# Splitting the product with C of a state-space scan between VectorE and GpSimd, and moving the gathers on GpSimd

## The reference, cut to what matters

```python
dA = jnp.exp(dt_t[..., None] * A)
h = dA * h + (dt_t * u_t)[..., None] * B_t[:, None, :]
y_t = jnp.einsum('bdn,bn->bd', h, C_t)
```

## Time and profile before

| what | value |
|---|---|
| median of three runs | 618.16 us (617.43 to 618.87) |
| the profiled execution | 619.79 us, its span 618.2 us |
| TensorE busy, its weight loads | 414.6 us, 206.4 us |
| VectorE busy | 477.4 us (77%) |
| ScalarE busy | 204.3 us (33%) |
| GpSimd busy | 351.2 us (57%) |
| from 125 to 345 us (most of the scan): VectorE busy | 209.6 of 220 us |

### The profile page before, as it was taken

One profiled execution on the slowest core, in us unless ns is written; L12 is line 12 of the kernel. 1 busy time (PEld: TensorE's weight loads), 2 busy tenths in 40 slices (PEclk: granted clock), 3 DMA queues, 4 the chain that ended last, 5 costly groups with the idle time before them and its releaser, 6 DMA issues.

```text
span 618.2 us, 8775 instructions
## 1 busy us (share of the span) xinstructions
PE 414.6 (67%) x3283; PEld 206.4 (33%) x3283; DVE 477.4 (77%) x625; ACT 204.3 (33%) x229; POOL 351.2 (57%) x307
## 2 busy tenths in 40 slices
PE   6786855757676677767767889687163996545751
PEld 2462323222232222222222345475132434522220
DVE  1999998799999999999998328999406469994242
ACT  2565992222323323333331355321011126112110
POOL 6667004569999999998998232889980000330000
PEclk7978976679999999999999999855556997567567
DMA  8540033925545475456440000000010000000000
GB/s 283 176 138 9 2 91 74 227 71 150 160 143 155 142 173 137 136 159 177 141 136 1 2 12 1 2 2 2 1 22 1 1 0 1 2 2 8 4 5 34
DMA packets 29523, 46.11 MB, mean 75 GB/s; under 512 B 18146, under 2 KB 19588, under 8 KB 28452
## 3 DMA queue, kind: packets, MB, share of 16 engines
q1 hardware_dynamic: 27044, 45.12, 26.7%
q0 software_dynamic: 2368, 0.37, 0.5%
q10 hardware_dynamic: 64, 0.00, 0.0%
HBM read 43.57 MB, written 1.11 MB: 72 GB/s over the span
## 4 chain that ended last, share of the span: by engine, by line
DVE 31%; POOL 31%; PE 20%; issue 12%; ACT 3%; DMA 2%; DVEq 1%; ACTq 0%; POOLq 0%; SPq 0%
POOL dBu L888 14%; POOL hit L872 7%; PE ps L2015 4%; POOL work L965 3%; POOL work L967 3%; DVE hC L1552 2%; PE ps L2338 2%; POOL work L954 2%; DVE hst L1531 2%; DVE hC L1322 2%; PE ps L2223 2%; DVE hC L1318 1%; PE ps L2507 1%; DVE work L1778 1%; PE ps L2137 1%
## 5 line engine op out<-in xcount | busy, mean ns | idle before, releaser
L1157 ACT ACTIVATE ps<-work,a_neg 128x1020 f32<-128x1020 f32 x64 | 71.2, 1115 | 154.3 <-DVE hst L1531 102.6
L2153 PE MATMUL ps<-hC,ident 128*128 128x512 f32 x256 | 121.9, 598 | 0.0
L1531 DVE TENSOR_TENSOR_SCAN hst<-ps,dBu 128x1024 f32<-128x1024 f32 x43 | 98.3, 2286 | 5.1 <-POOL dBu L888 3.8
L2137 PE MATMUL ps<-late,pick_state 96*128 96x512 bf16 x128 | 40.0, 395 | 70.3 <-DVE hC L1552 68.9
L872 POOL DMA_INDIRECT hit<-in_L_attn_edge_values,tab_i x64 | 67.6, 1056 | 30.0 <-DMA hit<-in_L_attn_edge_values,tab_i 20.7
L888 POOL TENSOR_TENSOR dBu<-work,dA 128x1024 f32<-128x1024 f32 x32 | 75.3, 2357 | 7.0 <-DMA dA<-b_rows_all 4.2
L2153 PEld LDWEIGHTS ps<-hC,ident 128*128 128x128 f32 x256 | 49.4, 193 | 43.3 <-issue 34.8
L888 POOL TENSOR_TENSOR dBu<-work,b_sb 128x1024 f32<-128x1024 f32 x16 | 39.6, 2473 | 38.7 <-DVE dA L1460 37.2
L1552 DVE TENSOR_TENSOR hC<-hst,ps 128x1024 f32<-128x1024 f32 x43 | 51.5, 1197 | 1.8 <-PE ps L2137 1.8
L1531 DVE TENSOR_TENSOR_SCAN work<-ps,dBu 128x1024 f32<-128x1024 f32 x21 | 48.0, 2286 | 1.8 <-POOL dBu L888 1.1
L1002 POOL TENSOR_TENSOR work<-work 128x1024 f32<-128x1024 f32 x3 | 5.7, 1911 | 75.0 <-DVE work L1787 75.0
(11 more groups left out here) (371 smaller groups left out, 832.4 us busy)
## 6 DMA issues: line engine op xcount, KB each, us to landing
dA<-b_rows_all SPq DMA_DIRECT2D x64, 256.0 KB, 4.1
b_sb<-b_rows_all SPq DMA_DIRECT2D x32, 256.0 KB, 4.3
work<-b_rows_all SPq DMA_DIRECT2D x32, 256.0 KB, 4.1
work<-in_L_attn_edge_index SPq DMA_DIRECT2D x6, 1024.0 KB, 6.4
dA<-in_L_attn_edge_index SPq DMA_DIRECT2D x1, 1024.0 KB, 5.2
dBu<-in_L_attn_edge_index SPq DMA_DIRECT2D x1, 1024.0 KB, 8.3
hit<-in_L_attn_edge_values,tab_i POOLq DMA_INDIRECT x64, 3.8
late<-work SPq DMA_DIRECT2D x12, 64.0 KB, 2.0
```

Of the source, the lines that this page charges most:

```text
L1157: nc.scalar.activation(dst[:, :, 1:], src[:, :, 1:], ACT.Exp, scale=a_neg[:, n:n + 1]).then_inc(dA_sb, 1)
L1531: V.tensor_tensor_scan(h_buf[i % 3], dA_ps[k], dBu[:, k, :], 0.0, ALU.mult, ALU.add).then_inc(scan_done, 1)
L2137: last = T.matmul(bank(2 + h), pick_state[:, n, :, :].rearrange("p v i -> p (v i)"), parts[:, j * NT + h * HALF:j * NT + (h + 1) * HALF], ...
L2153: last = T.matmul(bank(6 + h), ident[:, :], hC[:, i % 2, h * HALF:(h + 1) * HALF], start=False, stop=(n == S - 1))
```

## The change

In 29 of the 64 states (every even one from 6 on, `SHARE_STEPS`) the product with C is split by columns. VectorE does the first 896 columns (800 in the last group), GpSimd the last 128 (224 in the last group). GpSimd reads no PSUM, so ScalarE copies these columns of C into one of three SBUF buffers that lie in the tile sq, not used in the scan (`state_out`, issued behind the exponential of the next state). GpSimd's part (`state_share`) stands behind dBu of two states on. Waits come with it: VectorE's product and TensorE's next spread of C wait for the copy, TensorE's addition and VectorE's scan three states on wait for GpSimd's part.

The gathers in the scan are now issued in the 30 odd states from 5 on, not 43. `EARLY` becomes 40, so that ten still lie between scan and window attention and eleven among the bands; the 13 that are left are issued behind the last band product, each waiting for the one before.

```diff
--- before.py
+++ after.py
@@ -137,9 +137,11 @@
         h_buf = [hst[:, 1, :], hst[:, 0, :], area(22, 1)]
         hC = sb("hC", [P, 2, NT])
         b_sb = sb("b_sb", [P, 2, NT])
-        EARLY = 2 * C - 11
-        GATHER_STEPS = [4, 5, 7, 8, 10, 11, 13, 14, 15] + \
-            [S * j + n for j in (1, 2) for n in range(14) if n % 3] + list(range(3 * S, J * S))
+        EARLY = 2 * C - 24
+        GATHER_STEPS = list(range(5, J * S, 2))
+        SHARE_STEPS = list(range(6, J * S, 2))
+        POOL_COLS = (128, 128, 128, 224)
+        c_sb = [sq[:, k * 256:(k + 1) * 256] for k in range(3)]
         b_buf = [b_sb[:, 0, :], area(4, 1), dA[:, 0, :], dA[:, 1, :]]
         b_rows = area(0, 1)
         b_dram = nc.dram_tensor("b_rows_all", [J, 2 * S, NT], F32, kind="Internal").ap()
@@ -480,6 +482,8 @@
         part_round = sem("part_round")
         c_in = sem("c_in")
         c_ps = sem("c_ps")
+        c_copied = sem("c_copied")
+        hc_pool = sem("hc_pool")
         y_ps = sem("y_ps")
         dA_zero = sem("dA_zero")
 
@@ -896,6 +900,16 @@
                 pool.wait_ge(dt_later, 4 * (j - 1) + quarter + 1)
                 link(nc.gpsimd.tensor_tensor(dtu[:, r], dt_act[:, r], u_act[:, r], ALU.mult))
 
+            def state_share(i):
+
+                k = SHARE_STEPS.index(i)
+                w = POOL_COLS[i // S]
+                pool.wait_ge(scan_done, i + 1)
+                pool.wait_ge(c_copied, k + 1)
+                pool.wait_ge(y_ps, i - 1)
+                nc.gpsimd.tensor_tensor(hC[:, i % 2, NT - w:], h_buf[i % 3][:, NT - w:], c_sb[k % 3][:, 0:w],
+                                        ALU.mult).then_inc(hc_pool, 1)
+
             state_input(0)
             state_input(1)
             for i in range(J * S):
@@ -906,6 +920,8 @@
                     pool.wait_ge(tab_dve, 1)
                 if i in GATHER_STEPS:
                     gather(GATHER_STEPS.index(i))
+                if i in SHARE_STEPS:
+                    state_share(i)
                 if j + 1 < J and n % 3 == 0 and n < 12:
                     later_delta(j + 1, n // 3)
             assert J * S == 2 * C
@@ -976,6 +992,9 @@
                 for i in islice(units_gathers, 2 if u % 3 == 1 else 1):
                     gather(i)
             window_bands(UNITS - 1)
+            for i in units_gathers:
+                pool.wait_ge(gathered, 16 * i)
+                gather(i)
             pool.wait_ge(gathered, 16 * 2 * C)
             nc.gpsimd.tensor_tensor(hit[:, :, 0, :], hit[:, :, 0, :], hit[:, :, 1, :],
                                     ALU.mult).then_inc(hit_sb, 1)
@@ -1168,8 +1187,19 @@
             for k in range(2):
                 last = nc.scalar.activation(turned[:, 2 * k:2 * k + 2, :], plane_pair(k), ACT.Copy)
             last.then_inc(turned_sb, 1)
+            def state_out(i):
+
+                k = SHARE_STEPS.index(i)
+                w = POOL_COLS[i // S]
+                act.wait_ge(c_ps, i + 1)
+                if k >= 3:
+                    act.wait_ge(hc_pool, k - 2)
+                nc.scalar.activation(c_sb[k % 3][:, 0:w], bank(2, 2)[:, NT - w:], ACT.Copy).then_inc(c_copied, 1)
+
             for i in range(2, J * S):
                 state_decay(i)
+                if i - 1 in SHARE_STEPS:
+                    state_out(i - 1)
             norm_steps(2, eps5)
 
 
@@ -1528,6 +1558,8 @@
                     dve.wait_ge(planes_t, 1)
                 if i >= 3:
                     dve.wait_ge(hc_done, i - 2)
+                if i - 3 in SHARE_STEPS:
+                    dve.wait_ge(hc_pool, SHARE_STEPS.index(i - 3) + 1)
                 V.tensor_tensor_scan(h_buf[i % 3], dA_ps[k], dBu[:, k, :], 0.0, ALU.mult,
                                      ALU.add).then_inc(scan_done, 1)
 
@@ -1549,7 +1581,11 @@
                 dve.wait_ge(c_ps, i + 1)
                 if i >= 2:
                     dve.wait_ge(y_ps, i - 1)
-                V.tensor_tensor(hC[:, k, :], h_buf[i % 3], bank(2, 2), ALU.mult).then_inc(hc_done, 1)
+                if i in SHARE_STEPS:
+                    dve.wait_ge(c_copied, SHARE_STEPS.index(i) + 1)
+                cols = NT - POOL_COLS[j] if i in SHARE_STEPS else NT
+                V.tensor_tensor(hC[:, k, 0:cols], h_buf[i % 3][:, 0:cols], bank(2, 2)[:, 0:cols],
+                                ALU.mult).then_inc(hc_done, 1)
                 if i == 1:
                     link(planes_to_table(tab[:, :], g_base[:, 0, :], link, turned, table_at))
                     table_indices(link).then_inc(tab_dve, 1)
@@ -2149,6 +2185,8 @@
                         T.matmul(bank(6 + h), skip_diag[:, :],
                                  u_act[:, j * NT + h * HALF:j * NT + (h + 1) * HALF], start=True, stop=False)
                 pe.wait_ge(hc_done, i + 1)
+                if i in SHARE_STEPS:
+                    pe.wait_ge(hc_pool, SHARE_STEPS.index(i) + 1)
                 for h in range(2):
                     last = T.matmul(bank(6 + h), ident[:, :], hC[:, i % 2, h * HALF:(h + 1) * HALF],
                                     start=False, stop=(n == S - 1))
@@ -2157,6 +2195,8 @@
             for i in range(J * S):
                 if i >= 1:
                     pe.wait_ge(hc_done, i)
+                if i - 1 in SHARE_STEPS:
+                    pe.wait_ge(c_copied, SHARE_STEPS.index(i - 1) + 1)
                 spread_c(i)
                 if i >= 1:
                     add_state(i - 1)
```

## The result

| | before, beside it | after |
|---|---|---|
| median of 4 runs | 618.51 us (617.43 to 619.87) | 625.62 us (623.16 to 627.67) |
| ratio | 1 | 1.0112, 95% interval 1.0066 to 1.0158 |
| the profiled execution, its span | 619.79, 618.2 us | 624.47, 622.8 us |

The change makes the kernel 1.1% slower. 618.8 was predicted, with a range of 616.0 to 621.8, so the forecast was wrong. The chain of waits by engine is the first view to read; it answers to the earlier trace rows.

What follows compares the result with a forecast made beforehand. The prediction took the chain's largest piece, the scan, as bound by VectorE at 3.32 us a state, with GpSimd's gathers and deltas lengthening steps. Scan -2.2 and tail +2.8 made +0.6 on 618.16: 618.8 us, range 616.0 to 621.8.

Steps and rivals of the forecast that it cites:

- The scan: 64-state scan: fewer gathers and shorter VectorE products against 29 GpSimd shares, net -2.2 us, between -4 and +1.5.
- The method: Scan: stepping VectorE's scans and GpSimd's dBu, each start at its later condition; 208.4 us against the trace's 208.2.
- The moved gathers: Behind the last band: 13 gathers at 3.02 us delay bias loads 39.4, disturbed gathers add 1.1; whole tail +2.8 us.
- the cover: Before VectorE's mask work: 38.7 us by which bias loads could come later without delaying it, used up to 0.7 beyond.
- The router's share of it: Tail: three gathers beside VectorE's router work contend with it, 0.3 us each, +1.0 us together.
- the rule on shared interfaces: Skill's rule: GpSimd contends with VectorE instructions in two-port mode or with two SBUF inputs; without it tail 1.8 us.
- The sum of the steps: Whole kernel: scan -2.2 and tail +2.8 give +0.6 us, two changes that cancel.
- The added waits: Scan: new waits for copy, share and spread of C are met in time and cost nothing, the copy with 1.0 us in hand.
- the four cases: Whole kernel: the prediction's alternatives 1 to 4; the first, both halves as written, net +0.6 us, 618.8, chance 0.42.
- Rival 3: Behind the bands: moved gathers decide, bias loads land late at pitches from 3.23 us on; 620.8 us, chance 0.22.
- Rival 2: Behind the bands: tail covered, gathers at quiet pitch, no collision; tail 0.4 to 1, net -1.8, 616.4 us, chance 0.28.
- Rival 4: Scan: the share doesn't pay since GpSimd sets the step; scan gains nothing, tail +2.8 alone, 621 us, chance 0.08.

Runs made afterwards that it cites:

- gonly: Kernel before with only the gathers moved (30 in the scan's odd states, 13 behind the bands), no share: 616.85 us, ratio 0.9968.
- sonly: Kernel before with the share in all 29 states, gathers left in the scan, two implied VectorE waits left out: 626.99 us, ratio 1.0148.
- best1: Changed kernel, shares only in the last group's eight even states (288 columns), implied VectorE waits dropped, two gathers moved ahead of window attention: 611.07 us, ratio 0.9897.
- lean: Changed kernel without its 57 added VectorE instructions, waits that others imply; same work and order: 618.18 us, ratio 1.0006.
- a71: Changed kernel with 71 more VectorE instructions in a never-taken branch ahead of the loop: 618.53 us, ratio 1.0013.
- pad57: Kernel before with 57 more VectorE instructions, met waits at its program's start, nothing else: 626.17 us, ratio 1.0109.
- padpa: Kernel before with 58 more met waits on TensorE and 55 on ScalarE at their programs' start, VectorE as before: 620.32 us, ratio 1.0036.

## Why the prediction was wrong

- **The scan, forecast -2.2, measured -2.4.** Both prices were right: the pitch of 0.42 us for a 128-column share, and a copy well under the 1.1 us at which the exponential would come late. The method held in every variant: gonly -4.1 (stepped -4.1), sonly +10.0 (+10), best1 -6.1 (-6.2). The steps had the groups right too: scans 16, 32, 48 and 63 come 0.7, 1.0, 0.3 and 2.4 us earlier, counted from scan 3, where 0.7, 1.1, 0.3 and 2.5 were forecast. What I passed over is that the sum has two parts of opposite sign, -4.1 from the gathers and +1.7 from the shares.
- **The moved gathers, forecast +39.4 and 1.1 on GpSimd, measured 41.05.** From the last band's end to the first store of the bias are 41.62 us (449.32 to 490.94) where 0.57 were (454.12 to 454.69). On the path this makes a wait of 0.56 us in the profiled execution, 2.65, 2.28 and 1.77 in lean, a71 and gonly. Forecast were 2.8. The spread comes from the cover: from the router's start to the mask work without the wait pass 36.2 us in after, 35.1 in lean, 34.5 in gonly. It is 34.5 in before too, and 36.1 in pad57 and in padpa, which moved no gathers. The cover goes roughly with the granted clock of that stretch: 34.4 to 34.6 at 0.85, 35.0 to 36.2 at 0.80 or 0.81, 37.9 in best1 at 0.73.
- **The router's share of it, forecast +1.0 for contention, is wrong.** GpSimd's gathers beside it took 0.94 to 1.14 us, and VectorE's steps keep their 0.42 of the earlier trace rows. The slow subtraction and gather from which I took it, by the rule on shared interfaces that the prediction cites, are no measure for steps of 256 columns. VectorE's timeline beside these gathers is below. The cover of gonly, with gathers beside its router, is before's 34.5.

```profile
468.53 0.42 DVE L1757 TENSOR_TENSOR work<-work,rank 128x256 f32<-128x256 f32 x1
468.99 0.42 DVE L1758 TENSOR_REDUCE top<-work 128x32 f32<-128x256 f32 x1
```

- **The sum of the steps, +0.6, was right for what they cover.** With VectorE's loop back at its place the change costs +0.6 us (lean, 618.18 against 617.55) or +0.8 (a71, 618.53 against 617.68). Neither can be told from nothing. That the sum agrees is in part luck: the router's 1.0 in it didn't come, and the cover moves by more than that between traces.
- **The step that failed is "The added waits".** I asked of each wait who stands behind it and whether it is met, and put the sum at nothing. I did not count the instructions that the waits are made of, nor ask which later code they move. What the runs showed in its place is three more stalls of 2.7 to 3.1 us in VectorE's loop. Each kernel taken against the one before beside it, the missing term is 6.3 us by a71 (7.1 less 0.8), 6.5 by lean (7.1 less 0.6), and 8.6 by pad57. None of the four cases had it. Rival 3, the slower one, gave 620.8 by pitches of 3.27 to 3.4 that didn't come (3.16). Rival 2's covered tail is half true, with a wait of 0.56 to 2.65. Rival 4 had the right suspicion for three of the four groups, but in the last one the share pays, and the gathers alone bring 4.1.

In the single traces 6.1 us show in the loop, and three stalls, each less the 0.25 of before, sum to 7.8. The loop without added stalls takes 49.8 to 53.0 us by trace, with the granted clock, so one trace does not fix the price better than this; the timed kernels put it between 6.3 and 8.6.

## What to carry to other kernels

Added waits cost code as well as time: count the instructions that a change adds to each engine ahead of a late loop or branch, and look in the chain for "issue" of some 3 us behind a jump and in the queues for more instruction packets. When a change of a few instructions moves the time by a per cent in a stage that it doesn't touch, run the kernel before with the same number of never-executed instructions beside it, and the change with as many more as fill a block (128 on VectorE here). A split of work onto a second engine pays only in the stretch where the first sets the pace; here that was one group of four.

## What the runs showed that I had not expected

- A taken jump to code that VectorE's sequencer has to fetch costs 2.7 to 3.8 us, against 0.25 where it doesn't. Its code comes in packets of 8 KB (queue q14), and a loop of some 390 instructions, of which 299 are jumped over, depends on its place modulo 128 instructions: a shift of 28 adds one stall, 57 three, 128 none.
- 57 waits that are met cost VectorE nothing visible at the start (scan 3 at 125.38 against 125.29), while 55 on ScalarE and 58 on TensorE, both put at the start, delay the same scan by 3.35 us. In the change, where they lie further on, scan 3 isn't late (124.65).
- Two-operand work of 256 columns on VectorE and gathers on GpSimd don't hinder each other (0.42 and 0.94 to 1.14 us); beside a band product on GpSimd the subtraction took 2.60.
